# State matmuls ahead of the transposes, out-projection three slots behind, masked product behind the convolution

## What is computed

```
h     = rmsnorm(layernorm(x))
gate, hBC, dt = split(h @ in_proj_w.T)            # 8192 gate, 8192 hidden + 2048 B and C, 128 dt
hid, B, C     = split(silu(causal_conv(hBC)))     # 4 taps
dt    = softplus(dt + dt_bias)
M     = (C @ B.T) * exp(segsum(-exp(A_log) * dt)) # per head, lower triangle ("decay" * "cbm")
y     = M @ (hid * dt) + Dp * hid
yg    = y * silu(gate)
out   = (yg * rsqrt(mean over the group of yg^2)) * gnorm_w @ out_proj_w.T
x     = x + layernorm(x) + out
```

## Time and profile before

| | us |
|---|---|
| median of 3 runs | 827.75 |
| the profiled execution | 823.68 |
| its span, first to last instruction | 821.9 |
| TensorE busy | 790.5 (96%) |
| VectorE busy | 612.4 (75%) |
| ScalarE busy | 603.8 (73%) |
| GpSimd busy | 615.7 (75%) |

### The profile page before, as it was taken

How to read it: one execution, slowest core, us unless ns; L and a number is a source line. 1 busy time by engine, 2 the same in 40 slices (tenths; PEclk the granted TensorE clock), 3 DMA queues, 4 the chain that set the end, 5 groups by cost and what they waited for, 6 DMA issues and landing times.

```text
span 821.9 us, 13293 instructions
## 1 busy us (share of the span) xinstructions
PE 790.5 (96%) x4319; PEld 610.7 (74%) x4322; DVE 612.4 (75%) x752; ACT 603.8 (73%) x1052; POOL 615.7 (75%) x552
## 2 busy tenths in 40 slices
PE   8799899999999999999999999999999999989897
PEld 7567677777777777777777777777777777767664
DVE  6768987777786867776786867776786867787774
ACT  5778786888688876878688886878688886877442
POOL 6669966799578986799578986799578985795231
PEclk9999999999999999999999999999999999999999
DMA  8433324334234324333233314334233324340001
GB/s 332 148 92 127 129 65 155 128 120 138 90 128 128 128 64 154 128 128 128 90 128 128 128 64 154 128 128 128 90 128 128 128 65 155 128 154 1 4 2 52
DMA packets 48812, 94.93 MB, mean 116 GB/s; under 512 B 3952, under 2 KB 36848, under 8 KB 48784
## 3 DMA queue, kind: packets, MB, share of 16 engines
q1 hardware_dynamic: 48496, 94.06, 34.6%
q10 hardware_dynamic: 288, 0.52, 0.2%
HBM read 93.26 MB, written 1.31 MB: 115 GB/s over the span
## 4 chain that ended last, share of the span: by engine, by line
PE 62%; DVE 17%; ACT 11%; issue 7%; DMA 0%; POOL 0%; ACTq 0%; DVEq 0%
PE ps_z L1093 19%; PE ps_out L1196 15%; PE ps_h L1093 13%; PE ps_y L1183 7%; DVE conv_bc L728 4%; DVE conv L728 4%; ACT decay L531 4%; PE ps_t L1066 2%; ACT L531 2%; ACT conv L477 2%; DVE v L846 2%; DVE yg L852 2%; DVE decay L786 2%; ACT conv_bc L461 1%; DVE y_lo L858 1%
## 5 line engine op out<-in xcount | busy, mean ns | idle before, releaser
L728 DVE SCALAR_TENSOR_TENSOR conv<-ps_h,w_raw,conv 128x510 f32<-128x510 f32 (+2 forms) x192 | 143.2, 746 | 102.1 <-ACT conv L477 97.6
L531 ACT ACTIVATE decay<-csx,cs_own 128x256 f32<-128x256 f32 (+1 forms) x512 | 184.4, 443 | 1.0
L297 POOL TENSOR_TENSOR win_lo<-w_raw,win_hi 128x1024 fp32r<-128x1024 f32 x64 | 153.1, 2392 | 0.9 <-DMA csx<-cs_rows 0.9
L399 POOL TENSOR_TENSOR sqacc<-sqacc,sq 128x512 f32<-128x512 f32 x47 | 69.8, 1486 | 107.1 <-ACT sq L567 107.1
L786 DVE TENSOR_TENSOR decay<-decay,cbm 128x1536 f32<-128x1536 f32 x64 | 126.0, 1969 | 3.6 <-ACT decay L531 3.6
L1183 PE MATMUL ps_y<-decay,hid_dt 128*64 128x256 f32 (+1 forms) x1024 | 98.9, 336 | 16.1 <-DVE hid_dt L835 16.1
L539 ACT ACTIVATE hidT<-conv 128x512 f32<-128x512 f32 x64 | 40.5, 633 | 100.5 <-DVE conv L728 100.5
L1183 PEld LDWEIGHTS ps_y<-decay,hid_dt 128*64 128x64 f32 x1024 | 64.1, 138 | 58.9 <-DVE hid_dt L835 21.8
L337 POOL TENSOR_SCALAR_AFFINE_SELECT csx<-csx 128x512 f32<-128x512 f32 x128 | 102.1, 823 | 0.5 <-DMA csx<-cs_rows 0.5
L1196 PE MATMUL ps_out<-wout_hi,y_lo 128*128 128x512 f32 x252 | 99.9, 396 | 0.0
L1196 PE MATMUL ps_out<-wout_hi,y_hi 128*128 128x512 f32 x252 | 99.5, 395 | 0.0
(11 more groups left out here) (314 smaller groups left out, 1514.2 us busy)
## 6 DMA issues: line engine op xcount, KB each, us to landing
w_raw<-in_wmain SPq DMA_DIRECT2D x64, 772.0 KB, 4.3
csx<-cs_rows SPq DMA_DIRECT2D x128, 256.0 KB, 3.5
bc_raw<-in_wbc SPq DMA_DIRECT2D x8, 517.0 KB, 3.5
ctx_raw<-in_ctx SPq DMA_DIRECT2D x1, 2048.0 KB, 16.2
bc_raw<-in_wffn SPq DMA_DIRECT2D x2, 512.0 KB, 3.8
out_x<-acc SPq DMA_DIRECT2D x4, 256.0 KB, 2.1
acc<-in_x ACTq DMA_DIRECT2D x2, 256.0 KB, 3.9
acc<-in_x SPq DMA_DIRECT2D x2, 256.0 KB, 3.7
```

Source lines behind the costliest of these rows:

```text
L297: eng.tensor_tensor(win_lo[:, r2, :], w_raw[:, r4, 0:W_IN], win_hi[:, r2, :].bitcast(f32), ALU.subtract).then_inc(low_win, 1)
L399: eng.tensor_tensor(sqacc[:], sqacc[:], sq[:, (k - 1) % 2, :], ALU.add).then_inc(pool_sq, 1)
L531: done = eng.activation(decay[:, r2, b, h, lo:lo + n], csx[:, r2, b, h, lo:lo + n], ACT.Exp, bias=cs_own[:, r2, t, h:h + 1])
L728: eng.scalar_tensor_tensor(out=out_b[:, :, back:], in0=src_b[:, :, 0:S - back], scalar=w[:, TAPS - 1 - back:TAPS - back], in1=out_b[:, :, ...
```

## The change

On TensorE the order in a slot becomes: hidden projection of pair s, gate projection of pair s, out-projection of pair s-3 (before: s-2), state matmuls of pair s-1, transposes of pair s. In k = 7 and 0 (`turned`) the out-projection stands ahead of the gate projection. The products of B and C write to `ps_h` and `ps_t` and stand ahead of the state matmuls; the column sums go to k = 2.

VectorE: `combine` and `lower_y` serve pair s-2 (before: s-1), `combine` comes first in the slot, the masked product serves pair s-1; it stands ahead of the convolution in k = 0, 1 and 7 and behind it in k = 2 to 6. `add_group` goes to k = 3. ScalarE: the exponentials are those of pair s and stand first, then `tap`, `finish_y` (pair s-2), `hidden`, `gates`. GpSimd: the sum of squares stands ahead of the splits (pair s-3), the split of the output weights is that of pair s and comes after `select`; rstd goes to k = 3. SyncE: the load of pair s still waits for `y_lo` of pair s-4, which VectorE now makes one slot later, and for that pair's `wout_lo`. Behind the slots stand two out-projections instead of one.

```diff
 # SyncE
                     if late(s - 3):
                         eng.wait_ge(dve_ylo, s - 3)
+                        eng.wait_ge(low_wout, s - 3)
                     eng.dma_start(w_raw[:, r, :], wmain_d[s]).then_inc(w_in[r], 16)
 # GpSimd
+                if k == 3 and not first:
+                    eng.wait_ge(dve_ms, g)
+                    eng.tensor_tensor(rstd[:], ms[:], half_neg[:], ALU.pow).then_inc(pool_rstd, 1)
                 if not (last and k == PPG - 1):
                     eng.wait_ge(w_in[n4], 16 * (2 * g + (k + 1) // 4 + 1))
...
-                    if late(s - 2):
-                        eng.wait_ge(pe_out, s - 2)
+                if late(s - 3):
+                    eng.wait_ge(pe_out, s - 3)
...
+                sum_squares(s, g, k, first)
                 if not (last and k == PPG - 1):
                     split_in(n4, (k + 1) % 2)
-                    split_out(n4)
                     eng.wait_ge(csx_in[1 - r2], 32 * (4 * g + (k + 1) // 2 + 1))
                     lower_in(n4, (k + 1) % 2, s + 2)
                     select(1 - r2)
-                    lower_out(n4, s + 2)
+                split_out(r4)
+                lower_out(r4, s + 1)
 # ScalarE
+                decays(s, k)
+                if k == PPG - 1 and not last:
+                    tap_bc(0, g + 1, ps_z, conv_bc[:])
...
-                if not (first and k == 1):
-                    tap(s, g, k)
-                hidden(s, k)
-                gates(s, k)
+                tap(s, g, k)
                 finish_y(s, g, k, first)
-                if not (last and k == PPG - 1):
-                    decays(s + 1, k + 1)
...
+                hidden(s, k)
+                gates(s, k)
 # VectorE
             def slot(eng, s, g, k, first, last):
-                r2 = k % 2
+                if not (first and k < 2):
+                    combine(s, k)
                 if not (first and k == 0):
                     scale_hidden(s, k)
-                if k == 2 and not first:
+                if k == 3 and not first:
                     add_group(g - 1)
+                early = k in (0, 1, PPG - 1)
+                if early and not (first and k == 0):
+                    mask(s, g, k)
                 if k == PPG - 1 and not last:
                     conv_group(0, g + 1, ps_z, conv_bc[:])
...
+                conv_hidden(s, k)
+                if not early:
+                    mask(s, g, k)
+                if not (first and k < 2):
+                    lower_y(s, k)
...
+            def mask(s, g, k):
+
+                eng.wait_ge(act_exp, s)
+                if k == 1:
+                    eng.wait_ge(dve_cb, 2 * g + 2)
+                q2 = (k - 1) % 2
+                eng.tensor_tensor(decay[:, q2], decay[:, q2], cbm[:].unsqueeze(2).broadcast_to([P, B, 2, MJ]),
+                                  ALU.mult).then_inc(dve_m, 1)
 # TensorE
+                turned = k == 0 or k == PPG - 1 and not last
...
                 project(ps_h[:], win_hi[:, r2, 0:KT * P], win_lo[:, r2, 0:KT * P], pe_hid)
                 if first and k == 0:
                     start_up()
+                if turned and not (first and k == 0):
+                    project_out(s, g, k)
...
+                project(ps_z[:], win_hi[:, r2, KT * P:], win_lo[:, r2, KT * P:], pe_gate)
+                if not turned and not (first and k < 3):
+                    project_out(s, g, k)
+                if k == 0:
+                    products_of_bc(s, g)
+                if k == 2 and not first:
+                    sum_channels(s, g - 1)
                 if not (first and k == 0):
                     scan_heads(s, k)
...
             slots(eng, slot)
+            project_out(PAIRS, GROUPS, 0)
             scan_heads(PAIRS, 0)
-            project_out(PAIRS, GROUPS, 0)
+            eng.wait_ge(low_wout, PAIRS - 1)
+            project_out(PAIRS + 1, GROUPS, 1)
```

More of the change, by code:

```diff
@@ L380, in slot @@
                     lower_bc(g + 2)
[L382 to L385, removed]
             def sum_squares(s, g, k, first):
-                if k == 1 or (first and k == 0):
+                n = (k - 3) % PPG
+                gs = g if k >= 3 else g - 1
+                if n == 0 or (first and k < 3):
                     return
[L391 to L394, removed]
+                eng.wait_ge(act_sq, s - 2)
+                if n == 1:
+                    if late(gs):
+                        eng.wait_ge(pe_ss, gs)
                     eng.tensor_tensor(sqacc[:], sq[:, 0, :], sq[:, 1, :], ALU.add).then_inc(pool_sq, 1)
                 else:
-                    eng.wait_ge(pool_sq, (PPG - 1) * g + k - 2 if k else (PPG - 1) * (g - 1) + PPG - 2)
-                    eng.tensor_tensor(sqacc[:], sqacc[:], sq[:, (k - 1) % 2, :], ALU.add).then_inc(pool_sq, 1)
+                    eng.wait_ge(pool_sq, (PPG - 1) * gs + n - 1)
+                    eng.tensor_tensor(sqacc[:], sqacc[:], sq[:, n % 2, :], ALU.add).then_inc(pool_sq, 1)
             slots(eng, slot)
+            sum_squares(PAIRS, GROUPS, 0, False)
+            sum_squares(PAIRS + 1, GROUPS, 1, False)
             eng.wait_ge(dve_ms, GROUPS)
@@ L499, in slot @@
                     decays(s, k)
-                    tap(s + 1, g, k + 1)
-                    decays(s + 1, k + 1)
                     return
+                if first and k == 1:
+                    tap(s, g, k)
+                    decays(s, k)
+                    scale_context(0)
+                    hidden(s, k)
+                    gates(s, k)
+                    return
+                decays(s, k)
+                if k == PPG - 1 and not last:
+                    tap_bc(0, g + 1, ps_z, conv_bc[:])
                 if k == 0:
                     tap_bc(1, g, ps_z, conv_bc[:])
[L505 to L508, removed]
-                if not (first and k == 1):
-                    tap(s, g, k)
-                hidden(s, k)
-                gates(s, k)
+                tap(s, g, k)
                 finish_y(s, g, k, first)
-                if not (last and k == PPG - 1):
-                    decays(s + 1, k + 1)
                 if first:
@@ L519, in slot @@
                     scale_context(PPG - 1)
+                if k == PPG - 1 and not last:
+                    silu_bc(0, g + 1, conv_bc[:])
+                if k == 0:
+                    silu_bc(1, g, conv_bc[:])
+                hidden(s, k)
+                gates(s, k)
             def decays(s, k):
@@ L1159, in slot @@
                     eng.wait_ge(dve_cb, 2 * g + 2)
-                if k == 1 and not first:
+                if k == 2 and not first:
                     eng.wait_ge(dve_ms, g)
@@ L1171, in slot, with products_of_bc @@
                             wbc_lo[:, which * KT * P:(which + 1) * KT * P], pe_bc)
+            def products_of_bc(s, g):
+                eng.wait_ge(act_bc, 2 * g + 2)
+                eng.wait_ge(dve_conv, 3 * s + 3)
+                if late(s):
+                    eng.wait_ge(dve_hiddt, s)
+                for b, bank in ((1, ps_h), (0, ps_t)):
+                    q = b * S
+                    mm(bank[:, 0:S], bcT[:, 0, q:q + P], bcT[:, 1, q:q + S], start=True, stop=True)
+                    mm(bank[:, S:MJ], bcT[:, 0, q + P:q + S], bcT[:, 1, q + P:q + S], start=True,
+                       stop=True).then_inc(pe_cb, 1)
             def scan_heads(s, k):
@@ L1188, in project_out @@
             def project_out(s, g, k):
-                pair, q2, q4 = (k - 2) % PPG, (k - 2) % 2, (k - 2) % 4
-                eng.wait_ge(dve_ylo, s - 1)
+                pair, q2, q4 = (k - 3) % PPG, (k - 3) % 2, (k - 3) % 4
+                eng.wait_ge(dve_ylo, s - 2)
                 for t in range(TT):
-                    if k == 2 and late(TT * g):
+                    if k == 3 and late(TT * g):
                         eng.wait_ge(dve_acc, TT * (g - 1) + t + 1)
```

107 lines of the change are left out of this document (43 added, 64 removed).

## The result

The changed kernel is slower: 857.18 us median (849.34 to 859.95, four runs) beside 827.4 for the kernel before in the same session, a ratio of 1.036 (95% interval 1.027 to 1.044). The forecast was 853. The profiled execution took 849.34 us with a span of 847.5, where the forecast had 847.1 for the span; it is the shortest of the four, so the trace shows the cheapest form of the loss. One of 19 executions of the kernel before in a later session took 1970.77 us; the ratios leave it out.

What follows compares the result with a forecast made beforehand. TensorE, busy 790.5 of 821.9 us, bounds the kernel before. Span 821.9 + 27 (loop) - 2.3 (first group) + 0.5 (end) = 847.1; with 1.8 and 4.1 on top, 853 us; forecast 840 to 866, full range 819 to 870.

Steps and rivals of the forecast that it cites:

- the circle: Loop: load, GpSimd, exponentials, tap, convolution, product, y_lo pass lateness on; weights arrive at +2.7; 5.1 us a group, taken as 4.5.
- the hand schedule: One group followed with the profiled durations, door to whoever asked first: waits 0.5, 1.5, 0.3, 2.0, 1.2, sum 5.5 us.
- The door: VectorE instructions with two SBUF operands and GpSimd's exclude each other; `win_lo` holds the product for 2.2 us in k = 4.
- ScalarE's start: Slots k = 2 to 6: exponentials from -0.35 for 2.88 us, tap at 3.15, product done at 8.0, 0.5 us left.
- The power in k = 3: rstd one slot later: add_group waits for it to about 1.8 of k = 3, covered by `scale_hidden`; cost nothing.
- The reordering of TensorE at nothing: Same number of matmuls, new order costed at 0; bounds 0.1 us a slot either way, 6 us in all.
- First group: TensorE's losses there 16.3 us before, 14.0 after: gain 2.3 with full clock kept, 0 if lost once more.
- Last group and end: Before 2.92 + 1.5 + 0.8, after 4.5 plus 1 for the context's quantisation: about 0, taken as +0.5 us.
- The rule and the row: Skill's exclusive lock would make yg in k = 3 wait for the power, sum 857; a row showed the power holding nothing.
- A: TensorE stays the bound if weights come early enough or the product precedes `win_lo`: span 806.7, 812.5 us; chance 0.22.
- B: Every slot k = 2 to 6 at 12.0 us, repeating itself: 7.4 us a group, 871 us; chance 0.07.
- C: Loop loses 1.5 to 2 us a group, gains of first and last group offset part: 825 to 838; chance 0.13.

## Why the prediction was right, step by step

**The sign and the circle: right, and shown.** "The weights arrive at +2.7 of slot s, in the very slot in which GpSimd splits them": GpSimd's waits in group 6 end at +2.4 in k = 2, +3.4 in k = 3 and +3.95 in k = 4; the hand schedule had 1.7 for k = 2 and 3.7 for k = 4. In k = 5, for which it said 5.7, GpSimd begins at +5.4 (664.18 behind 658.77). Breaking the circle at the load brings back 32 us, and closing it in the old order costs 91, slower matmuls included.

**The door: right as a mechanism, with luck in who came first.** The schedule let `win_lo` start 0.15 ahead of the product and hold it for 2.2; it started 0.35 ahead and held for 2.05 (3.66 us for 1.75). But `win_lo` began at +6.50, where the schedule had 6.1, and won only because the product was later still, for the reason in the next paragraph. With the exponentials on time the product comes first, by 0.12 us (the rows above). The prediction had said that the wait would then turn up one slot later, "the same to 0.3 us"; the groups of that run take 97.9 to 99.2 us, 1.6 to 2.9 more than the 96.3 here, part of it slower matmuls (TensorE busy 800.4 us for 787.3).

**ScalarE's start: wrong.** "At -0.35 of its slot: 2.88 us of exponentials, then tap at 3.15." The matmuls do free ScalarE there, at -0.26, but the table load of 1.28 us follows, the exponentials start at +1.04 and `tap` at +3.83. The product asks at +6.85, not 6.25, and its 1.75 us end at 8.6, where the state matmuls want it at 8.55. The 0.5 us of slack that the prediction counted was not there. I had read the row of the exponentials, not the one ahead of it: the same load was there at 442.13.

**The sizes of the waits.** In group 6, in us:

| | forecast | measured |
|---|---|---|
| k = 3, ahead of the state matmuls | 0.5 | 0.89 |
| k = 4, the same | 1.5 | 1.98 |
| k = 5, the same | 0.3 | 0.98 |
| k = 6, ahead of the hidden projection | 2.0 | 0.38 |
| k = 6, ahead of the state matmuls | 1.2 | 0.62 |
| sum | 5.5 | 4.85 |

(0.38: from the start of the transposes to that of the projection 0.79 us pass at this border, 669.80 to 670.59, and 0.41 at the one before, 658.36 to 658.77.)

The step that failed and its consequence cancel in part. The product is late by 1.5 us more than forecast over k = 3, 4 and 5; a TensorE so delayed then reaches `win_lo` of the next pair at nearly the time it is done (0.38 for 2.0). That this is one trade and not two accidents is what the run with the table load ahead shows: the wait of k = 4 goes, that of k = 5 falls to 0.5 or 0.6, and the one for `win_lo` in k = 6 comes back, at 3.5 us. The groups lengthened by 3.9 to 4.3 us (3.5 for the first in the loop), where I had taken 4.5; six of them 24.3 us for 27.

**The power in k = 3: a term put at nothing.** The wait of k = 3 is not the table load's, since it stays without it. "rstd one slot later (add_group waits for it to about 1.8 of k = 3, covered by `scale_hidden`)" had the power end at 1.8. It ended at +2.70 of k = 3 (group 6, from 634.92), and VectorE stood still for it:

```profile
637.66 2.73 DVE L890 SCALAR_TENSOR_TENSOR acc<-ps_out,rstd,acc 128x512 f32<-128x512 f32 x4 [0.32 <-POOL rstd L356]
...
640.30 2.30 DVE L736 SCALAR_TENSOR_TENSOR conv<-ps_h,w_raw,conv 128x510 f32<-128x510 f32 x3
```

`tap` was done at 639.51; the convolution waited for the four additions until 640.30, and so the product came late.

**The reordering of TensorE at nothing: right.** 91.48 us busy in group 6 for 91.78. k = 0 is 0.4 us shorter (11.62 for 12.05), inside the bounds given.

**First group: the number right, by luck.** Group 1 begins 2.0 us earlier (119.30, before 121.27), for a gain of 2.3. But one out-projection of 12 matmuls, 2.8 us by the earlier trace rows (450.64 to 453.44), has moved from the first group to behind the slots (TensorE has 450 matmul records there, before 461), and the forecast of 2.3 was worked out from waits and clock alone. In these the first group got 0.8 us worse. The waits came about as forecast, 14.5 us for 14.0: 2.03 at the products (2.1 forecast), 0.74 for the copy (0.5), 2.04 for the silu of pair 1 (2.3), 4.09 for the product of pair 1 (3.4), then 2.0, 0.2, 1.5 and 1.9. (The 1.5 us that the kernel before lost at the products of the second group, counted in the forecast, lie outside the 2.0.) What was wrong is "full clock kept":

```profile
52.20 2.83 PE L1207 MATMUL ps_y<-decay,hid_dt 128*64 128x256 f32 x16 [4.09 <-issue]
```

2.83 us for 1.52, as behind the 4.11 us stall of the earlier trace rows; the granted clock was 0.83 from 50 to 60 us, for 0.66 in the ten of the earlier trace rows. The forecast itself had said 0 for this case.

**Last group and end: 3.3 for 0.5.** It took 149.8 us from the start of group 7, before 146.4. Of the 3.3, 2.8 are, by the same estimate, the out-projection moved there; without it the 0.5 is met. The prediction named the move but put no figure on it. The waits ahead of the state matmuls are as long as in the loop (1.71 and 1.89 us the longest), and the projection of k = 6 waits 1.49 for `win_lo`; what the context's quantisation has in it wasn't separated.

**The sum.** The span was met to 0.4 us (847.5 for 847.1) because errors cancel: the loop cost 2.7 less than taken, and the two ends 3.1 more (+1.3 for -1.8), the moved out-projection netting to nothing between them. The closeness is luck; the direction and the circle behind it are not.

**The rule and the row.** I let the power on four columns hold nothing, and had 857 as the sum by the Trainium skill's rule ("SBUF — State Buffer", section "SBUF: two separate sides"). This is the very place that the rule spoke of, yg in k = 3 (group 5 of the changed kernel, GpSimd's `wout_lo` and power, then VectorE):

```profile
539.08 1.29 POOL L303 TENSOR_TENSOR wout_lo<-w_raw,wout_hi 128x512 fp32r<-128x512 f32 x1
540.33 1.47 POOL L356 TENSOR_TENSOR rstd<-ms,half_neg 128x4 f32<-128x4 f32 x1
```

```profile
539.41 1.51 DVE L866 TENSOR_TENSOR yg<-v,gate 128x512 f32<-128x512 f32 x1
```

yg is held by `wout_lo` until 540.37 and ends at 540.92, in the middle of the power, which runs to 541.80. Here yg had asked first, so the row tests only whether yg keeps the power waiting. It does: in the traces of this case the power on four columns took 1.46 to 1.53 us wherever yg had asked before it, and 1.01 to 1.03 everywhere else. Whether the power holds yg is shown where the power starts first. Group 1 of the kernel before, GpSimd, then VectorE:

```profile
142.76 1.01 POOL L385 TENSOR_TENSOR rstd<-ms,half_neg 128x4 f32<-128x4 f32 x1
```

```profile
142.79 0.71 DVE L852 TENSOR_TENSOR yg<-v,gate 128x512 f32<-128x512 f32 x1 [0.49 <-DVE v L846]
```

yg starts 0.03 behind the power and takes its plain 0.7 us. So the power holds nothing, as the earlier trace rows had it, and the trace speaks against the rule for this instruction on that side. On the other side it agrees: the power is itself held, by 0.45 us. That I had overlooked, and it is a part of the lateness in k = 3 told above. That the median came to 857.18, the sum by the rule, is no support for the rule: the median lies 7.8 us above the profiled execution, where I had taken 4.1. For wide instructions the rule holds: product 3.66 us, `y_lo` 2.84, `win_lo` 3.73 where plain ones took 1.75, 0.74 and 2.4.

**The rivals.** A (TensorE stays the bound, 806.7 of span) is what the kernel does once the load is early and the product first: 808.0. Its condition, weights at +1.0 or earlier, was the right one, and its other half, the product slipping in ahead, is needed as well: with the load alone it is 825. Against the kernel before, that version gains 5.1 us in the first group, 2.1 in the second, 0.5 to 0.6 in each of the next four, 1.6 in the last of the loop and 2.9 behind it, 13.9 in all. But A's parts came out otherwise: with the moved out-projection put back, the first group gains 2.3 and the end 5.7 (A had 8 and 5.2), the loop 6.0 (A had 2). B did not occur: in the loop k = 4 took 12.3 to 13.8 us, but k = 3 and 5 only 10.9 to 11.9, and no state repeated from slot to slot. C did not either; the early load alone lands at its lower edge.

## What to carry to other kernels

When a step is moved one slot back, look for everything that waits for it as "the last reader": here a subtraction that used one parameter column of a tile kept 772 KB of weights from being loaded, and a tile of their own for the small parameters was worth 32 us. When work moves from one stretch to another, book it in both, or a gain in one and a loss in the other will look like waits. Two defects of a schedule may hide each other: product first and table load ahead were worth nothing or less with late weights, so mend what sets the pace (the load) first and try the rest again behind it. When an instruction moves behind a wait, read in the timeline what the engine did directly ahead of it, a table load for instance, since that moves behind the wait too.

## What the runs showed of the hardware

- **The table load goes with the activation, behind its wait.** 1.28 us, 63 times; in the old order it ran while ScalarE had nothing to wait for (1.1 us idle ahead of all 63), in the new one ScalarE was idle for 150.2 us ahead of them and the load came after. A one-column exponential ahead of the wait brings it forward. The page of the changed kernel:

```profile
L538 ACT ACT_TABLE_LOAD x63 | 80.8, 1283 | 150.2 <-PE ps_y L1207 136.1
```

And of the kernel with the exponential of one column:

```profile
L534 ACT ACT_TABLE_LOAD x63 | 80.8, 1283 | 1.1
```

- **Gaps and the clock.** Behind waits of up to 2.06 us in the changed kernel the state matmuls took 1.52 us as ever. Behind 2.21 us, in k = 4 of groups 3 and 4, they took 1.67 and 2.30, with a granted clock of 0.83 over the ten us from there; behind 4.09 us they took 2.83. The length of the gap alone doesn't decide: in the kernel before, behind 3.36 us, they took 1.52 at a granted clock of 1.00. One row of each kernel, changed and before:

```profile
464.44 2.30 PE L1207 MATMUL ps_y<-decay,hid_dt 128*64 128x256 f32 x16 [2.21 <-issue]
```

```profile
87.21 1.52 PE L1183 MATMUL ps_y<-decay,hid_dt 128*64 128x256 f32 x16 [3.36 <-DVE hid_dt L835]
```

Behind 3.53 us, in the kernel with the product first, the first four matmuls ran plain and the later ones at the lower of the two levels for a while; each row is four matmuls, and the third takes 1.10 us elsewhere:

```profile
576.88 1.19 PE L1110 MATMUL ps_h<-hT_hi,win_hi 128*128 128x512 f32 x4 [3.53 <-POOL win_lo L298]
577.90 1.56 PE L1110 MATMUL ps_h<-hT_lo,win_hi 128*128 128x512 f32 x4
579.26 1.91 PE L1110 MATMUL ps_h<-hT_hi,win_lo 128*128 128x512 f32 x4
```

The granted clock over the ten us from there was 0.83. This goes with the fact that one wait of 3.5 us in a group was no cheaper than 4.8 in pieces: the groups of that kernel took 97.2 us, those of the changed one 96.3, and its TensorE was busy 800.1 us for 787.3.
